# A mixture-of-experts stage re-tiled: two hidden tiles by 1024 tokens, with the second product's weights held in the array and its output turned

## The reference

```
scores = x2 @ Wr + br                      # 2048 x 8
share  = softmax over the two best of 8, 0 for the others
y      = sum over e of share[:, e] * (relu(x2 @ W1[e] + b1[e]) @ W2[e] + b2[e])
out    = layernorm(x2 + y)                 # W1[e] 256 x 1024, W2[e] 1024 x 256
```

## Time and profile before

| | |
|---|---|
| time before, 3 runs | 1701.66 us median (1701.38 to 1706.99) |
| the profiled execution, its own time | 1698.96 us |
| its span, first to last instruction | 1697.2 us |
| mean granted TensorE clock | 0.990 of 2.4 GHz |
| instructions | 33804 |

### The profile page before, as it was taken

The page is one execution under the profiler, slowest core; times in us unless marked ns, Lnnn a source line. Parts: engine busy times, 40 slices in busy tenths (PEclk is TensorE's granted clock), DMA queues, the critical chain, the costliest instruction groups (busy, mean ns, idle before and its releaser), DMA issues.

```text
span 1697.2 us, 33804 instructions
## 1 busy us (share of the span) xinstructions
PE 1633.6 (96%) x11448; PEld 1342.9 (79%) x11448; DVE 1166.4 (69%) x3826; ACT 835.6 (49%) x2768; POOL 1040.7 (61%) x1461
## 2 busy tenths in 40 slices
PE   6899999999999999999998799999999999999998
PEld 5586786776777868767776489999999999999997
DVE  4568767877787678777775588567556665657557
ACT  1566947948758579488486632222222222222221
POOL 2566756847657567477475677566666565657553
PEclk9899999999999999999999899999999999999999
DMA  7203003012031030120211020001010101010001
GB/s 220 66 2 84 19 25 78 2 45 57 2 74 28 16 86 2 45 57 2 65 32 51 2 69 29 28 1 50 1 50 1 51 1 50 1 51 1 1 1 50
DMA packets 52460, 63.54 MB, mean 37 GB/s; under 512 B 12288, under 2 KB 40448, under 8 KB 52160
## 3 DMA queue, kind: packets, MB, share of 16 engines
q1 hardware_dynamic: 51568, 58.62, 12.5%
q10 hardware_dynamic: 720, 2.75, 0.5%
HBM read 29.89 MB, written 2.10 MB: 19 GB/s over the span
## 4 chain that ended last, share of the span: by engine, by line
PE 77%; POOL 6%; DVE 6%; ACT 6%; issue 5%; DMA 0%; DVEq 0%; POOLq 0%; ACTq 0%
PE ps_Y L2246 21%; PE ps_H L2246 20%; PE ps_S L1450 17%; PE ps_O L1450 5%; ACT pr L890 5%; PE ps_X L1450 5%; PE ps_T L1679 4%; POOL pr L726 3%; PE ps_T L1450 2%; PE ps_T L1799 1%; POOL rot L666 1%; PE ps_S L1799 1%; DVE sm L1361 1%; POOL rot L676 1%; DVE h_hi L2209 1%
## 5 line engine op out<-in xcount | busy, mean ns | idle before, releaser
L2034 POOL TENSOR_TENSOR h_lo<-h_sb,h_hi 128x512 fp32r<-128x512 f32 x256 | 363.5, 1448 | 107.1 <-DVE h_hi L2209 107.1
L2080 ACT ACTIVATE h_sb<-ps_H,b_sb 128x512 f32<-128x512 f32 x256 | 176.7, 690 | 503.7 <-PE ps_H L2246 475.5
L691 POOL TENSOR_TENSOR pr<-pr,rden 128x128 f32<-128x128 f32 (+2 forms) x768 | 307.2, 436 | 85.3 <-DVE rden L1242 84.9
L2209 DVE CAST h_hi<-h_sb 128x512 fp32r<-128x512 f32 x256 | 247.0, 985 | 122.4 <-ACT h_sb L2080 122.2
L890 ACT ACTIVATE pr<-sm,nmx 128x128 f32<-128x128 f32 (+2 forms) x768 | 311.8, 414 | 23.1 <-DVE nmx L1253 23.0
L2246 PE MATMUL ps_Y<-w_hi,h_lo 128*128 128x256 f32 x1024 | 286.5, 280 | 0.0
L2246 PE MATMUL ps_Y<-w_hi,h_hi 128*128 128x256 f32 x1024 | 286.5, 280 | 0.0
L2246 PE MATMUL ps_Y<-w_lo,h_hi 128*128 128x256 f32 x1024 | 286.4, 280 | 0.0
L726 POOL TENSOR_TENSOR pr<-pr,rden 128x256 f32<-128x256 f32 x256 | 150.6, 615 | 111.1 <-DVE rden L1242 110.8
L1253 DVE CUSTOM_DVE_ANT_0 sm<-ps_S,cmask 128x128 f32<-128x128 f32 (+2 forms) x768 | 192.6, 308 | 33.9 <-PE ps_S L1450 25.0
L2246 PE MATMUL ps_H<-x_hi,w_hi 128*128 128x512 f32 x512 | 199.8, 390 | 0.0
(11 more groups left out here) (265 smaller groups left out, 3121.2 us busy)
## 6 DMA issues: line engine op xcount, KB each, us to landing
qT_sb<-rot SPq DMA_DIRECT2D x256, 64.0 KB, 2.0
w_raw<-in_W SPq DMA_DIRECT2D x16, 1024.0 KB, 6.2
kT_sb<-rot SPq DMA_DIRECT2D x192, 64.0 KB, 2.0
xin<-in_x SPq DMA_DIRECT2D x8, 256.0 KB, 2.8
cin<-in_ctx SPq DMA_DIRECT2D x8, 256.0 KB, 2.7
w_kw<-in_wink ACTq DMA_DIRECT2D x2, 768.0 KB, 5.8
w_ks<-in_selk SPq DMA_DIRECT2D x2, 768.0 KB, 5.5
out<-x SPq DMA_DIRECT2D x3, 512.0 KB, 3.1
```

Source lines behind the costliest of these rows:

```text
L691: last = pool.tensor_tensor(p_, p_, rden[:, h % 2, n:n + 1].to_broadcast([P, width]), ALU.mult)
L2034: pool.tensor_tensor(h_lo[:, s % 2, ht, :], h_sb[:, ht % 4, :], h_hi[:, s % 2, ht, :].bitcast(F32), ALU.subtract).then_inc(lo_sb.sem, 1)
L2080: ins = act.activation(h_sb[:, ht % 4, :], pst[plan.bank(f)][:, :], ACT.Relu, bias=b1[:, 2 * i + s // NCH, ht:ht + 1])
L2209: dve.tensor_copy(h_hi[:, s % 2, ht, :], h_sb[:, ht % 4, :]).then_inc(hi_sb.sem, 1)
```

## The change

The expert stage is rewritten; the attention stage keeps its code. The work is cut in 64 quads: expert `e`, half `p` of the tokens (1024), and `q`, a pair of hidden tiles (`q` and `q + 4`). A quad has 4 hidden tiles of 128 units by 512 tokens. PE issues `hidden_dense(g)`, `outputs([g - 1])`.

- Second product: now the weights (`w_hi`, `w_lo`) are stationary and `h_hi`/`h_lo` move, 512 columns each. Out come 128 channels by 512 tokens. The four banks Y0 to Y3 hold 2 token blocks by 2 channel halves, and build up over the four quads of a block (24 matmuls per quad, 6 per bank).
- Hidden tile: ACT reads the bank twice, once into `h_hi` and once into `h_sb`; DVE's cast is gone. POOL's subtraction stays. The hidden bank is only given back after both. `h_hi`/`h_lo` hold two quads.
- Output: since partitions are now channels, the share differs along the free axis. The shares are turned on PE (`turned_shares`), copied out by ACT, written to DRAM (`shares`) and read back, copied to all 128 partitions, 1024 tokens at a time (`load_share`, 16 DMAs of 512 KB). Per block DVE does 4 operations (Y + b2) * share on 128x512 from the banks, and from expert 1 on 4 additions of 128x512 to `total`, both `output_pair`.
- Weights: single-buffered. DVE and POOL overwrite the slices of expert `e` by those of `e + 1` one at a time, once PE is through with a slice (`high_slice`, `low_slice`; two 128x512 pieces each, in quads 8e+6 to 8e+9).
- End: `total` is turned back by PE (32 transposes of 128x128, `turn_total`, 8 groups), added to `x2` by DVE (`add_turned`, 16 additions), and normalised. Groups 0 to 3 go in quads 61 and 62. Quads 62 and 63 share one accumulation, bank after bank: Y0 to Y2, then groups 4 and 5 are turned, then Y3, then groups 6 and 7. Eight token tiles are then normalised singly instead of four.
- Arena: `w_lo0`, `turned` and `b2` move; `share` takes the place of `b2`, `small` moves out of it.

The core of the diff (routing, loads and names cut):

```diff
+        DENSE = 2 * NQ
+        RING = 2
             def rectify(g, k, src):
+                if k == 0 and g >= RING:
+                    act.wait_ge(y_part, y_bank(g - RING, 3))
+                act.activation(h_hi[:, g % RING, k, :], src, ACT.Relu, bias=bias)
+                act.activation(h_sb[:, k, :], src, ACT.Relu, bias=bias).then_inc(rect_sb, 1)
...
             def output(s, b):
+                dve.wait_ge(y_part, y_bank(NQ * s + NQ - 1, b))
+                return dve.scalar_tensor_tensor(to, pst[f"Y{b}"][:, :], b2[:, e, o:o + 1],
+                                                share[:, s % 2, CH * n:CH * n + CH], ALU.add, ALU.mult)
...
             def high_slice(e, q):
+                dve.wait_ge(raw_in, 32 * e)
+                dve.wait_ge(y_part, y_bank(DENSE * (e - 1) + NQ + q, 3))
...
-                    for tt in range(TT):
-                        for ht in range(NHT):
-                            row = slice(C * (ht % 4), C * (ht % 4) + C)
-                            terms += split_terms(
-                                (h_hi[:, s % 2, ht, tok], w_hi[e][:, 2 + ht // 4, row]),
-                                (h_lo[:, s % 2, ht, tok], w_lo[e][:, 2 + ht // 4, row]))
-                            last = mm(pst[plan.bank(f)][:, 0:C], a, b, n == 0, n == len(terms) - 1)
+                    col = slice(C * q + P * o, C * q + P * o + P)
+                    for m in range(2):
+                        terms += split_terms((w_hi[:, 2 + m, col], h_hi[:, g % RING, 2 * m + n, :]),
+                                             (w_lo[:, 2 + m, col], h_lo[:, g % RING, 2 * m + n, :]))
+                    last = mm(pst[f"Y{b}"][:, :], x, y, q0 == 0 and k == 0, q1 == NQ - 1 and k == len(terms) - 1)
...
+            for g in (QUADS - 3, QUADS - 2):
+                hidden_dense(g)
+                outputs([g - 1], range(2))
+                pe.wait_ge(rect_sb, tiles_of(g, 4))
+                pe.wait_ge(total_done, 4 * (STEPS - 1))
+                for group in ((0, 1) if g == QUADS - 3 else (2, 3)):
+                    turn_total(group)
+                outputs([g - 1], range(2, 4))
+            hidden_dense(QUADS - 1)
+            last = [QUADS - 2, QUADS - 1]
+            outputs(last, range(3))
+            pe.wait_ge(rect_sb, tiles_of(QUADS - 1, 4))
+            pe.wait_ge(total_done, 4 * (STEPS - 1) + 2)
+            for group in (4, 5):
+                turn_total(group)
+            outputs(last, [3])
+            pe.wait_ge(total_done, 4 * STEPS)
+            for group in (6, 7):
+                turn_total(group)
```

More of the change, by code:

```diff
@@ L1912, in attention_stage, with expert_stage @@
     return HandOver(banks, (x2_sb.sem, x2_sb.at(last, 1)), s_split0_hi, s_split0)
-def expert_stage(nc, outer, block, sh, ends, w, out):
+def expert_stage(nc, outer, block, sh, ends, w, shares, out):
     ctx = outer
@@ new lines, in _ @@
+            sp.wait_ge(rt_out, 1)
+            sp.dma_start(shares.rearrange("e (t p) -> (e t) p", p=P), rt_turned).then_inc(s_kept, 16)
+            sp.wait_ge(s_kept, 16)
+            load_share(0)
+            load_share(1)
+            for e in range(1, NE):
+                for s in (2 * e, 2 * e + 1):
+                    sp.wait_ge(y_read, 4 * (s - 1))
+                    load_share(s)
+                if e + 1 < NE:
+                    sp.wait_ge(w_low, slices(e, NQ - 1))
+                    load(e + 1)
@@ L2047, in _, with low_slice @@
[L2047 to L2050, removed]
+            def low_slice(e, q):
+                pool.wait_ge(w_high, slices(e, q))
+                cols, rows_ = slice(P * q, P * q + P), slice(C * q, C * q + C)
+                pool.tensor_tensor(quarters(w_lo)[:, :, cols], quarters(w_raw)[:, :, cols],
+                                   quarters(w_hi)[:, :, cols].bitcast(F32), ALU.subtract).then_inc(w_low, 1)
+                pool.tensor_tensor(w_lo[:, 2:4, rows_], w_raw[:, 2:4, rows_], w_hi[:, 2:4, rows_].bitcast(F32),
+                                   ALU.subtract).then_inc(w_low, 1)
@@ new lines, in outputs, with add_turned @@
+            def outputs(s):
+                if s == 0:
+                    dve.wait_ge(s_b2, 16)
+                else:
+                    dve.wait_ge(total_done, 4 * s)
+                dve.wait_ge(share_in[s % 2], 16 * (s // 2 + 1))
+                output_pair(s, 0)
+                output_pair(s, 1)
+            def add_turned(group):
+                dve.wait_ge(turn_full, group + 1)
+                bank = turned_bank(group)
+                for tt in range(2):
+                    t = 2 * group + tt
+                    dve.tensor_tensor(x2[:, t, :], pst[bank][:, C * tt:C * tt + C], x2[:, t, :], ALU.add
+                                      ).then_inc(turn_read, 1)
@@ new lines, in high_slice @@
+            def high_slice(e, q):
+                dve.wait_ge(raw_in, 32 * e)
+                dve.wait_ge(y_part, y_bank(DENSE * (e - 1) + NQ + q, 3))
+                cols, rows_ = slice(P * q, P * q + P), slice(C * q, C * q + C)
+                dve.tensor_copy(quarters(w_hi)[:, :, cols], quarters(w_raw)[:, :, cols]).then_inc(w_high, 1)
+                dve.tensor_copy(w_hi[:, 2:4, rows_], w_raw[:, 2:4, rows_]).then_inc(w_high, 1)
+            for g in range(QUADS):
+                e, p, q = quad(g)
+                if g == 1:
+                    last_rows()
+                if g == 2:
+                    route()
+                if q == 0 and g:
+                    outputs(g // NQ - 1)
+                if slice_after(g):
+                    high_slice(*slice_after(g))
+                if g == QUADS - 3:
+                    add_turned(0)
+                    add_turned(1)
+                    dve.wait_ge(turn_read, 4)
+                    variances(range(0, TT))
+                if g == QUADS - 2:
+                    add_turned(2)
+                    add_turned(3)
+                    dve.wait_ge(turn_read, TILES2)
+                    variances(range(TT, TILES2))
+                    normalise(range(0, TT), 0)
@@ new lines, in _ @@
+            normalise(range(TT, TILES2), 1)
+            last = STEPS - 1
+            dve.wait_ge(total_done, 4 * last)
+            dve.wait_ge(share_in[1], 16 * NE)
+            output_pair(last, 0)
+            dve.wait_ge(total_done, 4 * last + 2)
+            output(last, 2).then_inc(y_read, 1)
+            for group in (4, 5):
+                add_turned(group)
+            for t in range(TILES2, TILES2 + TT):
+                dve.wait_ge(turn_read, t + 1)
+                variances([t])
@@ L2349, in _, with bank_given_back, passes @@
-            turns(pe, turn)
+            def bank_given_back(bank):
+                f = (("x2T", 0), ("x2T", 1), "scores", "route")[bank]
+                pe.wait_ge(pre.free_sem(f), pre.after(f, 0))
+            def passes(bank, pieces):
+                terms = [x for hi, lo in pieces for x in split_terms(hi, lo)]
+                for n, (a, b) in enumerate(terms):
+                    last = mm(pst[f"H{bank}"][:, :], a, b, n == 0, n == len(terms) - 1)
+                last.then_inc(full[bank], 1)
@@ new lines, in hidden_dense @@
+            def hidden_dense(g):
+                e, p, q = quad(g)
+                if g == 0:
+                    pe.wait_ge(ends.split_lo, 2)
+                if e and p == 0:
+                    pe.wait_ge(w_low, slices(e, q))
+                for k in range(4):
+                    if (g, k) == (4, 3):
+                        pe.wait_ge(rt_out, 1)
+                    if g == 0:
+                        given_up(pe, f"S{k}")
+                    else:
+                        pe.wait_ge(rect_sb, tiles_of(g - 1, k + 1))
+                    if g > QUADS - 3 and k % 2:
+                        pe.wait_ge(turn_read, 4 * (g - QUADS + 3))
+                    row = slice(CH * (k // 2) + P * q, CH * (k // 2) + P * q + P)
+                    tok = slice(CH * (2 * p + k % 2), CH * (2 * p + k % 2) + CH)
+                    passes(k, [((w_hi[:, c, row], x_hi[:, c, tok]), (w_lo[:, c, row], x_lo[:, c, tok]))
+                               for c in range(NC)])
@@ new lines, in outputs, with turned_shares @@
+            def outputs(gs, banks=range(4)):
+                s, q = gs[0] // NQ, gs[0] % NQ
+                pe.wait_ge(low_sb, tiles_of(gs[-1], 4))
+                if gs[0] == 0:
+                    pe.wait_ge(ends.split_lo, 4)
+                for b in banks:
+                    if q == 0 and s == 0:
+                        bank_given_back(b)
+                    elif q == 0:
+                        pe.wait_ge(y_read, 4 * (s - 1) + b + 1)
+                    output(gs, b)
+            def turned_shares():
+                pe.wait_ge(s_rt, 1)
+                pe.wait_ge(rect_sb, tiles_of(3, 4))
+                pe.transpose(pst["H3"][:, 0:P], rt[:, :, :].rearrange("p e t -> p (e t)"), ident[:, :]).then_inc(rt_full, 1)
@@ new lines, in turn_total @@
+            def turn_total(group):
+                for tt in range(2):
```

(29 more changed lines are left out.)

331 lines of the change are left out of this document (127 added, 204 removed).

## The result

Twelve timed runs of each: before 1700.07 us median (1697.05 to 1706.99), after 1714.83 us (1708.11 to 1724.53). The ratio is 1.0075, with a 95% interval of 1.0055 to 1.0095: 12.8 us slower, 9.4 to 16.1 by the interval (the medians are 14.8 us apart). The forecast was no change, 1701.6 us.

A forecast was written before the change was run, and what follows sets the result against it. PE, busy 96% of the span, was taken as the bound. Last matmul: 1690.2 - 11.5 - 2.4 + 0.3 + 2.4 + 3.3 = 1682.3; plus 14.8 gives 1697.1 us of span, like for like 1701.6; range 1696 to 1707.

The forecast's parts named there:

- the price of the second product: Second product on PE: 1536 matmuls of 512 columns at 227.3 ns, 349.1 us in place of 360.6, 11.5 us gained.
- Slower: Whole kernel: the outcome of a time above 1710.2 us, outside the 0.5% band for no change; chance 0.21.
- the outer one: Time of the whole kernel: the wider range, 1691 to 1715 us, reaching to the cheap end and the two slow rivals.
- The line through the two rows: PE's matmul price: 227.3 ns at 512 columns and 117.4 at 256 imply 7.5 ns per matmul whatever its width.
- the rival with 234.8 ns: Second product: wide matmuls bring no gain, a column costs what it did in outputs; +11.5 us, 1713; chance 0.06.
- The rule of 2.5 ns beyond the columns: Matmul price on PE: columns at 2.4 GHz plus about 2.5 ns, so the wide second product would save only 3.8 us.
- Hidden tiles: ACT's two passes and POOL's h_lo per quad: ready at about +3.3 us, wanted at +10.9; 7.6 us of slack.
- Weight slices: Overwriting weights at quad 8e+8: slice ready at T + 5.5 us, wanted at T + 10.9; cost 0, cover 5 us.
- The rival: Weight slices late: DVE additions of 1.9 us make PE wait, 13 us on six experts, 1714; late hand-overs 0.12.
- Seam: Router and shares at the expert stage's start: router's wait goes, 2.4 us gained; turning shares costs 0.3; their DRAM trip hidden.
- End: After hidden(63): PE waits 3.3 us for h_lo, last matmul at F + 15.1, span ends 29.9 us after F.
- The tail behind the last matmul: DVE's work and the DMA after PE's last matmul: 14.8 us where it was 7.0; not about 15 would be wrong.

## Why the prediction was wrong

**The step that failed** is the price of the second product: "The nearest row is the first product: same type, same 512 columns, same 128x128 stationary: 227.3 ns." The two share all that, but not where the moving operand lies against the stationary one, which the prediction left out. The price is 233.5 ns: 64 x 5.60 = 358.4 us in place of 349.1, so 2.2 us gained and not 11.5. The first product rose by some 0.025 us a quad, 1.6 in all. Together that is 10.9 us, and the quads say the same: 64 x 11.08 = 709.1 us where 349.1 + 349.1 = 698.2 was forecast. The expert stage came out at 732.9 where 1697.1 - 974.3 = 722.8 was forecast: 10.1 too long. Moving `h` to the same place, with only the tensors behind it moved along, takes 12.1 us off; that was shown. The timed ratio, 12.8 us, holds the 10.1 within its interval of some 3.4 us either way.

"Slower" had been given 0.21 in all. The result lies outside the forecast's own range, 1696 to 1707 us, and only just inside the outer one, 1691 to 1715.

The line through the two rows that were to support the 227.3 ("256 columns more cost 109.9 ns, which leaves 7.5 ns") proves nothing, since any two numbers fit a line, and both depended on placement: with another gap the 117.4 becomes 119.9, and beside a second product that reads `x` the 227.3 becomes 226.7. With the operands alike in both kinds of row, the same line gives 226.7 - 119.9 = 106.8 ns for 256 columns more and 13.1 left over, not 7.5. And the rival with 234.8 ns, given 0.06, had the right price within 1.3 ns for a reason that did not hold, which is luck: wide matmuls do gain, at 226.7 ns 1536 x (2 x 117.4 - 226.7) = 12.4 us.

The rule of 2.5 ns beyond the columns (the Trainium skill, TensorE: Matmul & The Clock Gate, "Back-to-back issue gap") lies below every row here, 215.8 ns for 512 columns against 226.7 at best. That section gives it for an isolated matmul, which the prediction passed over, and 131 ns for a matmul of 512 columns in a stream of load and matmul pairs; no run here comes near that either. The same page of the Trainium skill ("Step-by-step: what each phase is for") has the weight load and the moving operand on ports of their own, so that loading does not take bandwidth from a running matmul. The runs differ from what one would read into that: with each matmul's load under way beside it, its cost changes by up to 6.8 ns with where the two operands lie against each other. The measurement decides here.

**Hidden tiles, right.** ACT rectifies twice: the two activations take 690 and 682 ns, POOL's subtraction 1298 (1448 before; DVE's casts beside it are gone, but that they were the reason was not tested), and PE waits for `h_lo` once, at the last quad:

```profile
L2071 POOL TENSOR_TENSOR h_lo<-h_sb,h_hi 128x512 fp32r<-128x512 f32 x256 | 330.9, 1298 | 257.1 <-ACT h_sb L2107 246.3
L2106 ACT ACTIVATE h_hi<-ps_H,b_sb 128x512 fp32r<-128x512 f32 x256 | 176.7, 690 | 370.7 <-PE ps_H L2291 346.5
```

**Weight slices, right.** This is POOL at a quad 8e+8 (start, us, what, idle before):

```profile
1170.89 1.75 POOL L2063 TENSOR_TENSOR w_lo<-w_raw,w_hi 128x512 fp32r<-128x512 f32 x1 [5.67 <-DVE w_hi L2237]
1172.59 1.29 POOL L2065 TENSOR_TENSOR w_lo<-w_raw,w_hi 128x512 fp32r<-128x512 f32 x1
```

The block's last outputs end at 1168.15 in the chain, so the slice is ready at T + 5.7, where 5.5 was reckoned. POOL does stand idle there for 5.67 us, and DVE makes two additions there in 1.28 us, 0.64 each and not 1.9. POOL waits like this 7 times, once for each expert but the first, and never longer than 5.7 us. The rival falls: POOL was idle at the slice, as was argued, and the additions were fast.

**Seam, right.** PE waits for nothing from its first hidden matmul to the last quad, neither at the router nor at the turned shares. From that matmul to the end of hidden(63) PE takes 1685.04 - 981.46 = 703.6 us, where 1682.3 - 15.1 - 974.3 = 692.9 was forecast: 10.7 too long. The two products account for all of it, so the other terms up to there hold.

**End, right in sum, and in part by luck.** This is PE at the last hidden quad and behind it:

```profile
1679.56 5.48 PE ps_H L2291 x24
...
1687.73 10.22 PE ps_Y L2291 x36
```

```profile
1704.98 1.09 PE L2396 MATMUL ps_H<-ident,total 128*128 128x128 f32 x8 [3.39 <-DVE total L2275]
```

F, the end of hidden(63), is 1685.04, the wait 2.7 (forecast 3.3), and the span ends at F + 29.4 (forecast 29.9). Two parts are off, against each other. After the wait the clock fell to its lower level, 1.2 GHz: it was granted in full up to 1688 us, 0.80 from there to 1690, 0.50 to 1692, 0.84 to 1694, then in full again. So 36 matmuls took 10.22 us where they take 8.42 without the wait, and the last matmul ended at F + 16.6 and not F + 15.1. The chain runs through these 36, so up to there nothing of the delay is hidden: DVE reads the third bank at F + 13.0, where F + 11.5 was reckoned. From then on DVE sets the end, and it took 16.4 us where 29.9 - 11.5 = 18.4 was reckoned: for instance four statistics took 2.96 us and not 3.4, four additions from a bank 1.32 and not 1.7. The tail behind the last matmul is 12.8 us, not 14.8, which the prediction itself had named as a sign of being wrong. These are DVE's last steps, answering to the earlier trace rows:

```profile
1710.33 0.42 DVE L2175 BATCH_NORM_STATS2 st<-x 128x6 f32<-128x256 f32 x1
...
1711.91 0.41 DVE L2187 TENSOR_SCALAR x<-x,mv,rstd 128x256 f32<-128x256 f32 x1 [0.44 <-POOL rstd L2080]
```

The shape of a tile's end is the same as before; there are eight of them now, and from 1698.04 us on DVE is never idle but for this one wait.

## What to carry to other kernels

When an operand changes its part, from stationary to moving, its place in memory has to be chosen anew: here 224 bytes of padding are worth 12 us of 733, more than the 11.5 that the wide second product was to bring. Take the price of a new kind of matmul only from a row whose operands lie against each other as the new ones will, or give the difference as a bound. And put ready work between the last producer and its consumer: at the end of a pipeline the cover of every other turn is missing, and here such work was worth 2.4 us.

## What was not expected of the hardware

The cost of a 512-column fp32r matmul with its own weight load hung here on the distance of the moving from the stationary operand within 256 bytes: 226.7 ns at 0, 256 and 512, 229.6 at 64, 232.9 at 128, 233.5 at 32. It is the distance that counts: with all operands moved by 32 bytes it is 226.7 again. With 256 columns and `h` stationary the order is another: 119.9 with `h` at 0, 117.8 at 64, 117.4 at 96. Distances of 96 and between 128 and 256 bytes with `h` moving were not run, nor 512 columns with the weights moving. Why it is so no run here shows, and that stays open.

The first matmuls of a phase can be dear as well: the first product took 5.48 us for 24 behind a second product at 32 off (its first 6 distances at 233 ns), and 5.44 behind one at 0. Lying alike is not all of it, since behind the 256-column second product at 0 the first product still took 10.91 us for 48, as in the kernel before, where 48 x 226.7 ns would be 10.88.
